# Attention's eight score pairs in three stretches of 2, 3 and 3 instead of four of 2, with all value products ahead of the last stretch

## What is computed

```python
q = _split_heads(hidden_states @ q_w.T + q_b)
k = _split_heads(context @ k_w.T + k_b)
v = _split_heads(context @ v_w.T + v_b)
scores = jnp.einsum('bhqd,bhkd->bhqk', q, k) / jnp.sqrt(jnp.float32(HD))
scores = jnp.where(mask, -jnp.inf, scores)
probs = jax.nn.softmax(scores, axis=-1)
ctx = jnp.einsum('bhqk,bhkd->bhqd', probs, v)
```

## Time and profile before

| what | before |
|---|---|
| median of 3 runs | 1226.94 us (1225.83 to 1227.11) |
| the profiled execution | 1227.52 us, its span 1225.7 us |
| PE busy | 1201.9 us, 98% of the span |
| PEld, DVE, ACT, POOL busy | 92%, 69%, 57%, 17% |
| chain that ended last | PE 85%, DVE 9%, ACT 3% |
| TensorE's granted clock | 0.998 of full speed |
| score matmuls (L986) | 768 of 64\*128, in 64 stretches |
| value matmuls (L948, 128x256) | 2496 |

### The profile page before, as it was taken

One profiled execution on the slowest core, in us unless ns is written; L12 is line 12 of the kernel. 1 busy time (PEld: TensorE's weight loads), 2 busy tenths in 40 slices (PEclk: granted clock), 3 DMA queues, 4 the chain that ended last, 5 costly groups with the idle time before them and its releaser, 6 DMA issues.

```text
span 1225.7 us, 25806 instructions
## 1 busy us (share of the span) xinstructions
PE 1201.9 (98%) x10197; PEld 1122.2 (92%) x10197; DVE 840.9 (69%) x2154; ACT 693.6 (57%) x1266; POOL 213.7 (17%) x239
## 2 busy tenths in 40 slices
PE   7999999999999999999999999999999999999997
PEld 6899999999999999999999999999778899899896
DVE  6656666666665666666565665676789878877877
ACT  6455545645644664564556456455655677676673
POOL 0004202310420251051033015101122000000012
PEclk9999999999999999999999999999999999999999
DMA  8102200320220031022003002200328676776763
GB/s 285 56 1 92 85 1 2 101 76 1 92 84 1 8 121 50 1 92 84 1 29 135 14 2 92 98 1 2 114 82 293 230 262 246 251 253 228 254 222 111
DMA packets 61060, 127.19 MB, mean 104 GB/s; under 512 B 3644, under 2 KB 21192, under 8 KB 60824
## 3 DMA queue, kind: packets, MB, share of 16 engines
q1 hardware_dynamic: 58776, 118.97, 28.1%
q0 software_dynamic: 2176, 6.72, 1.6%
HBM read 120.01 MB, written 14.32 MB: 110 GB/s over the span
## 4 chain that ended last, share of the span: by engine, by line
PE 85%; DVE 9%; ACT 3%; DMA 1%; issue 1%; SPq 0%; ACTq 0%; DVEq 0%
PE ptp L948 25%; PE work L948 22%; PE work L1335 7%; PE ptp_pv L1118 6%; PE work L986 6%; PE work L1337 3%; PE ptp L1358 2%; PE ptp L1361 2%; PE ptp L1359 2%; PE ptp L1360 2%; PE ptp L1362 2%; DVE kk_lo L1498 2%; ACT kk_hi L687 1%; DVE w_lo L1710 1%; PE work L1101 1%; DVE pt L1617 1%
## 5 line engine op out<-in xcount | busy, mean ns | idle before, releaser
L948 PE MATMUL ptp<-vw_hi,cx_hi 128*128 128x256 f32 x832 | 241.7, 291 | 0.0
L948 PE MATMUL ptp<-vw_lo,cx_hi 128*128 128x256 f32 x832 | 235.3, 283 | 0.0
L948 PE MATMUL ptp<-vw_hi,cx_lo 128*128 128x256 f32 x832 | 235.3, 283 | 0.0
L948 PE MATMUL work<-cx_hi,kw_hi 128*128 128x400 f32 (+1 forms) x504 | 175.5, 348 | 0.5 <-DVE cx_lo L1519 0.5
L948 PE MATMUL work<-cx_hi,kw_lo 128*128 128x400 f32 (+1 forms) x504 | 173.5, 344 | 0.0
L948 PE MATMUL work<-cx_lo,kw_hi 128*128 128x400 f32 (+1 forms) x504 | 173.2, 344 | 0.0
L948 PEld LDWEIGHTS ptp<-vw_hi,cx_hi 128*128 128x128 f32 x832 | 159.1, 191 | 13.9 <-issue 12.8
L948 PEld LDWEIGHTS ptp<-vw_lo,cx_hi 128*128 128x128 f32 x832 | 159.2, 191 | 0.0
L948 PEld LDWEIGHTS ptp<-vw_hi,cx_lo 128*128 128x128 f32 x832 | 159.2, 191 | 0.0
L1498 DVE SCALAR_TENSOR_TENSOR kk_lo<-work,biasT,kk_hi 128x400 fp32r<-128x400 f32 (+1 forms) x128 | 79.5, 633 | 115.5 <-ACT kk_hi L687 115.4
L687 ACT ACTIVATE kk_hi<-work,biasT 128x400 fp32r<-128x400 f32 (+1 forms) x128 | 75.2, 596 | 128.6 <-PE work L948 125.1
(11 more groups left out here) (301 smaller groups left out, 2596.8 us busy)
## 6 DMA issues: line engine op xcount, KB each, us to landing
w1raw<-in_w SPq DMA_DIRECT2D x32, 1024.0 KB, 5.2
w2raw<-in_w SPq DMA_DIRECT2D x32, 1024.0 KB, 7.1
raw<-in_ctxT SPq DMA_DIRECT2D x31, 832.0 KB, 6.5
pr<-in_mask SPq DMA_DIRECT2D x8, 800.5 KB, 4.3
xrow<-x_rows SPq DMA_DIRECT2D x7, 256.0 KB, 5.7
y_rows<-y_out_rows POOLq DMA_DIRECT2D x7, 256.0 KB, 2.6
xs<-in_x SPq DMA_DIRECT2D x1, 1024.0 KB, 9.4
qwraw<-in_qwT SPq DMA_DIRECT2D x1, 1024.0 KB, 9.2
```

The lines of the kernel that those rows point to most:

```text
L948: last = pe.matmul(dst, lhs(i, c), rhs(j, c), start=(c == 0 and (i, j) == (0, 0)), stop=(c == n - 1 and (i, j) == (1, 0)))
```

## The change

`SCORE_WINDOWS` cuts the eight pairs into stretches of 2, 3 and 3. The banks of a stretch are counted from 0: pairs go to `work` 0/1, `work` 2/3 and, the third, to the two banks of the sums (`ring = work + sums`), which are empty between the folding of one half's sums and the next half's first `weigh`. The order of PE becomes s s, v0 v1 v2, s s s, v3 v4 v5 v6, s s s, t, k0 to k5, w, k6 k7, w: all value items come before the last stretch, and `t` follows it directly. The two tiles turned in `t` go to the value banks (pair 2) instead of the banks of the sums (pair 3), so `turn` waits for the last value item, and tile 2 for tiles 0 and 1. The first `weigh` of a half now also waits until the third pair's banks are drained, and the third pair waits for `pv_free`. Exponential 3 (`e[3:]`) moves from behind v6 to behind k0. In the last half the special place for the turned tiles on DVE goes. The numbers of matmuls, copies, DMAs and exponentials are unchanged.

```diff
-        s = [[("s", 4 * h + 2 * i + rt, j) for j in (2 * u, 2 * u + 1) for rt in range(2)]
-             for i in range(2) for u in range(2)]
+        pairs = [[("s", 4 * h + 2 * i + rt, j) for rt in range(2)] for i in range(2) for j in range(NKC)]
+        s = [sum(pairs[low:high], []) for low, high in SCORE_WINDOWS]
...
-            steps += s[0] + v[0:1] + norms[0:1] + v[1:2] + s[1] + e[0:1] + v[2:3] + norms[1:2] + e[1:2] + v[3:4]
-            steps += norms[2:] + s[2] + v[4:6] + s[3] + t
+            steps += s[0] + v[0:1] + norms[0:1] + v[1:2] + norms[1:2] + v[2:3] + s[1] + e[0:1] + v[3:4] + e[1:2] + v[4:5]
+            steps += norms[2:] + v[5:] + s[2] + t
...
-            steps += v[6:] + e[2:] + turned + w[:1] + queried + w[1:]
+            steps += e[2:] + turned + w[:1] + queried + w[1:]
             continue
-        steps += s[0] + v[0:2] + s[1] + e[0:1] + v[2:3] + e[1:2] + v[3:4] + s[2] + v[4:6] + s[3]
-        steps += t + e[2:3] + v[6:] + e[3:]
+        steps += s[0] + v[0:3] + s[1] + e[0:1] + v[3:4] + e[1:2] + v[4:] + s[2] + t + e[2:3]
...
-            steps += k[:6]
+            steps += k[:1] + e[3:] + k[1:6]
...
+SCORE_WINDOWS = [(0, 2), (2, 5), (5, 2 * NKC)]
...
-PAIR_OF = [3, 3, 2, 0, 1, 2, 0, 1, 2, 1, 2, 0, 1, 2]
+PAIR_OF = [2, 2, 2, 0, 1, 2, 0, 1, 2, 1, 2, 0, 1, 2]
...
-            banks.append(scored % 4)
+            banks.append(scored)
             scored, others, late = scored + 1, 0, False
-        elif kind == "w":
+            continue
+        scored = 0
+        if kind == "w":
...
+        ring = work + sums
...
                 pe.wait_ge(w_free, before_bank(b, last, both[1]))
+                if bank_of(last, both[0]) == 4:
+                    pe.wait_ge(pv_free, 4 * b + 2 * (a // 4) + 1)
...
                 if jj == 0:
-                    pe.wait_ge(pv_free, 4 * b + 2 * h + 1)
+                    pe.wait_ge(w_free, count(b, last, ("v", h, TPH - 1)))
                 if jj == 2:
-                    pe.wait_ge(w_free, count(b, last, ("v", h, TPH - 1)))
+                    pe.wait_ge(pt_lo, NPT * b + j + PTD)
...
+                if j % (2 * TPH) == 0:
+                    pe.wait_ge(w_free, before_pair(b, last, 2, ("w", g, 0)))
```

More of the change, by code:

```diff
@@ L70, in steps_of @@
             norms = [("m", 0, j) for j in range(EARLY)]
-            steps += s[0] + v[0:1] + norms[0:1] + v[1:2] + s[1] + e[0:1] + v[2:3] + norms[1:2] + e[1:2] + v[3:4]
-            steps += norms[2:] + s[2] + v[4:6] + s[3] + t
+            steps += s[0] + v[0:1] + norms[0:1] + v[1:2] + norms[1:2] + v[2:3] + s[1] + e[0:1] + v[3:4] + e[1:2] + v[4:5]
+            steps += norms[2:] + v[5:] + s[2] + t
             turned, queried = [("n", 0, j) for j in range(EARLY)], [("q", 0, m) for m in range(EARLY_Q)]
-            steps += v[6:] + e[2:] + turned + w[:1] + queried + w[1:]
+            steps += e[2:] + turned + w[:1] + queried + w[1:]
             continue
-        steps += s[0] + v[0:2] + s[1] + e[0:1] + v[2:3] + e[1:2] + v[3:4] + s[2] + v[4:6] + s[3]
-        steps += t + e[2:3] + v[6:] + e[3:]
+        steps += s[0] + v[0:3] + s[1] + e[0:1] + v[3:4] + e[1:2] + v[4:] + s[2] + t + e[2:3]
         if last:
             a, r = [("a", 0, j) for j in range(EARLY)], [("r", 0, j) for j in range(EARLY)]
-            steps += k[:1] + a[:1] + k[1:2] + r[:1] + a[1:2] + k[2:3] + r[1:2] + a[2:] + k[3:4] + r[2:] + k[4:5] + [("l", 0, 0)] + k[5:6]
+            steps += k[:1] + e[3:] + a[:1] + k[1:2] + r[:1] + a[1:2] + k[2:3] + r[1:2] + a[2:] + k[3:4] + r[2:] + k[4:5] + [("l", 0, 0)] + k[5:6]
         else:
-            steps += k[:6]
+            steps += k[:1] + e[3:] + k[1:6]
         steps += w[:1] + k[6:] + w[1:]
@@ L204, in before_bank @@
     other = max(m for m in range(len(RING[0])) if BANKS[0][m] == bank)
-    return NW * b + FIRST_K + max(ITEMS[0].index(RING[0][other]) + 1 - NW, bank - 3)
+    return NW * b + FIRST_K + max(ITEMS[0].index(RING[0][other]) + 1 - NW, min(bank - 3, 0))
 def before_pair(b, last, pair, weighed):
@@ L985, in score_pair @@
                         rows = slice(2 * HD * rt, 2 * HD * (rt + 1))
-                        ins = pe.matmul(wide(work[bank_of(last, both[rt])], k), qbd[i][rows, cc, :],
+                        ins = pe.matmul(wide(ring[bank_of(last, both[rt])], k), qbd[i][rows, cc, :],
                                         kk[j][rows, cc, keys(k)], start=(i, j) == (0, 0), stop=(i, j) == (1, 0))
@@ L1009, in item @@
                 kind, a, k = step
-                bank = (ptp if spare(step) else work)[bank_of(last, step)]
+                bank = (ptp if spare(step) else ring)[bank_of(last, step)]
                 if kind == "s":
@@ L1643, in body @@
                     kind, a, j = step
-                    for i in turns(step) if not (last and step == ("t", 2, 0)) else ():
+                    for i in turns(step):
                         pt_item(b, last, i)
@@ L1661, in body @@
                         item(b, last, step)
-                    if last and step == ("v", 1, TPH - 1):
-                        for i in turns(("t", 2, 0)):
-                            pt_item(b, last, i)
                     if step == ("s", 3, NKC - 1):
```

## The result

The changed kernel takes 1253.13 us (median of 6 runs, 1250.15 to 1255.28), against 1226.17 of the kernel before in as many: 1.0218 times as long, with an interval of 1.0208 to 1.0229. That is 27 us more, where +0.4 was forecast. The profiled execution took 1253.41 us, its span 1251.6 us, 25.9 more than before.

What follows compares the result with a forecast made beforehand. PE, busy for 1201.9 of 1225.7 us, was taken as the bound. First halves -2.7, second halves +1.9 and the last sequence +1.2 gave +0.4 us on the median 1226.94: 1227.3 us, range 1222.5 to 1232.

Steps and rivals of the forecast that it cites:

- One switch less in every half: PE goes between full-array and half-array matmuls four times a half instead of five, saving 0.38 us in all 16 halves.
- Nothing waits in the first halves: First halves: DVE runs 1.0 us later after the last stretch, yet nothing waits; net -0.38 in seven halves, -2.7 us.
- t's wait for v6: PE's t waits for v6's low part; v6 ends 1.8 us before t, its copies take about 0.9; no stall forecast.
- ACT's queue behind chunk 3: Seven second halves: ACT idles 3 us for chunk 3's load, k4 waits, 0.65 us in all; net +0.27 each, +1.9.
- The last sequence: At two points where PE already waits for DVE, DVE comes 0.6 us later each; +1.2 us, bounds 0 and 2.0.
- the sentence on POOL's chunks: Second halves: POOL's chunks 2 and 3 end by 127 us, ahead of k4 and k6 that need them; no cost.
- the one on the slower side: Rival, chance 0.12: chunk 3's load takes 6.5 us, not 4.6, delaying k4 by +1.9 in seven second halves; 1240.6 us.
- three pairs make the emptying of banks the bound everywhere: Rival, chance 0.05: PE waits for DVE's emptying of banks in all 16 halves, +0.6 each, +9.6; 1236.5 us.

Runs made afterwards that it cites:

- the second experiment: Changed kernel with one wait more: POOL starts chunk 3's low part only when DVE has finished the query blocks; 1227.59 us, 1.0011 of the kernel before.
- the first experiment: Changed kernel with ACT's copy of context chunk 3 moved from behind v6 to behind k2; 1221.95 us, 0.9969 of the kernel before.
- the fifth experiment: Changed kernel with POOL's four value-bias additions of the fourth sequence moved behind the last group's sums; 1248.91 us.
- the fourth experiment: Changed kernel with four stretches of two pairs again, all values ahead of the last stretch, t behind it; 1250.01 us, 1.0191 of the kernel before.
- the third experiment: Kernel before with only DVE's query blocks of the second halves moved behind v6's low part; 1240.58 us, 1.0116 of the kernel before.

## Why the prediction was wrong

**One switch less in every half: right.** Forecast 0.38 us a half, 52.5 for a first half; measured 0.39 and 52.52.

**Nothing waits in the first halves: right.** None of the new waits shows; t's wait for v6, the one called thin, does not either.

**ACT's queue behind chunk 3: right as a mechanism and in size, where it is alone.** Forecast were 3 us of idle ACT, 0.45 us of idle PE and 53.2 us a half; the second experiment has 3.18, 0.49 and 53.26, and 1227.6 us as a whole, where 1227.3 was forecast. Against the kernel before beside it that is +1.0 us, where +0.4 was forecast.

**The last sequence: right in size, one wait in another place.** Forecast +0.6 us twice; measured +0.6 and +0.9, the second of them down to the end of the program, a stretch that varies by 1.7 us over the traces of the experiments on the changed kernel. In the first half PE waits 1.01 us for k0's low part, as forecast. In the last half it waits 2.16 us for DVE's low part of `t`'s second tile (`pt_end`), at 891.84, and 0.74 for its copies (`hT`), where it was one wait of 1.93 for `hT`. The forecast was one wait for `hT` of 2.5 us or more. The wait for `pt_end` is the new one of tile 2 for tiles 0 and 1, which the prediction had priced at nothing.

**The step that failed is the sentence on POOL's chunks.** I followed POOL's chunk 3 only forward, to its reader ("POOL's chunks 2 and 3 end by 127 us, ahead of k4 and k6 that need them"), and asked nothing of what runs beside it. By the prediction's own numbers it starts at 121.5 + 1.67 = 123.2 us, and the query blocks, 1.0 us later than before, run there from 122.7 to 124.9. Before, chunk 2 ended at 120.7, the blocks ran from 121.67 to 123.89, and chunk 3 began at 124.53. I priced the blocks at their duration in a place where POOL was silent. The missing term is 3.3 us in five second halves (56.6 against 53.26), made of about 1.7 more of idle PE (2.16 against 0.49) and 1.5 for the lower clock, which the prediction had at nothing too; 7.6 in the fourth; and 1.5 in the first, from the chunk that landed late: 16.5 + 7.6 + 1.5 = 25.6, the distance between the changed kernel and the second experiment (25.5).

Of the rivals, the one on the slower side had the right place in the queue but another mechanism; it came true only in the first sequence, by 1.5 us, and there against the prediction's argument that a late chunk shares its time with other chunks or the mask: no other context chunk was on its way then, as none was in the second sequence, where the chunk landed after 4.6 us. That three pairs make the emptying of banks the bound everywhere is refuted by the first experiment.

The Trainium skill has the rule that I did not set against the change: SBUF — State Buffer, section Who interferes with whom, says that VectorE and GpSimd share a pair of SBUF ports under an exclusive lock, that a copy or cast in a two-port mode contends for it, that an instruction with two SBUF inputs contends with GpSimd's reads, and that the one that issues second is fully blocked. The traces agree that casts and subtractions are both held; in which mode the casts ran they do not show. They agree on the order: in all 26 meetings with chunk 3, over the four traces that have them, one DVE instruction is held, it starts 0.03 to 0.26 us after POOL's, and it ends 0.07 to 0.15 us after POOL's end. Once the two start at the same time, in the first sequence of the fifth experiment at 124.46 us; there the subtraction takes its usual 0.29 us and POOL's takes 3.98 instead of 3.77 to 3.83. They agree on the converse too: a subtraction with one input in PSUM and one in SBUF took its usual 0.42 us at 223.35, in the middle of POOL's 7.54.

The collision theory as I put it ("DVE's instructions whose operands all lie in SBUF stand still") is too wide. In the kernel before, DVE's last steps to a row's maximum, SBUF to SBUF with one input each, run in the middle of POOL's chunk 0 and keep their length. DVE, then POOL:

```profile
106.91 0.16 DVE L1606 TENSOR_REDUCE nmx<-smx 128x1 f32<-128x4 f32 x1
107.11 0.15 DVE L1610 TENSOR_SCALAR nmx<-nmx 128x1 f32<-128x1 f32 x1
```

```profile
105.40 3.80 POOL L594 TENSOR_TENSOR cx_lo<-raw,cx_hi 128x1664 fp32r<-128x1664 f32 x1 [4.73 <-ACT cx_hi L674]
```

What the runs show as held are the casts of 32x128 and the subtractions with two inputs in SBUF.

## What to carry to other kernels

When a change moves work in time, do not only follow it to its readers. List what each engine that it touches now runs at the same moment, DVE's casts and two-input SBUF instructions against POOL above all, and see whether the two already ran together in the trace before. A duration that was read where the neighbour was idle is known only for that case. A reordering that saves something can be kept when the copy that it drags along is put back by hand: moving one copy behind k2 turned +2.2% into -0.3%.

## What the runs showed of the hardware

- A cast of 32x128 elements from SBUF to SBUF, 0.20 to 0.23 us by itself, or a subtraction of that size with both inputs in SBUF, 0.28 to 0.29 us by itself, lasted 3.71 to 3.88 us when it started just after a POOL subtraction of 3.8 us. It was one instruction each time, not all four. Taking the meeting away brought 1253 to 1228 us; bringing it into the kernel before, 1227 to 1241.
- Beside a POOL addition of 1.28 us (5.11 for four) four such subtractions took 1.24 to 1.27 us each, in the fourth sequence.
- Not held beside POOL were subtractions with one input in PSUM (0.42 us), and the reduction and the scalar operation of 128x1 from SBUF to SBUF (0.16 and 0.15 us).
- A wait of PE of 2.16 us was followed by some 3.3 us in which its matmuls ran at 1.2 GHz, and this cost the half 1.5 us. The length of the wait alone does not decide: of the fifth experiment's waits those of 2.12 us (second sequence) and 2.21 us (fourth) were followed by a fall of the clock and that of 2.18 us (sixth) was not; in the fourth experiment one of 1.83 us was (the granted clock was 0.58 and 0.56 in the next two stretches of 2 us) and another of 1.83 us, in the first sequence, was not. All waits of 1.29 to 1.31 us in the third experiment left it full. What decides stays open here.
- The same load of 832 KB landed after 4.6 us in the second sequence and after 6.2 us in the first of the changed kernel; in the fifth experiment it was 5.9 in the first again, in the second 4.8 us. Why is open too.
